# A two-call attention block with its feed-forward projections: a new deal of projection triples to slots, a score lag of four, two value visits, and earlier turns of the maxima

## Chip, cores and metric
One core of a Trainium2 chip. The metric is the device time of one execution in microseconds (us). The kernel of before took 627.68 us in the median of three runs.

## The reference, cut to what matters
The program computes two layers over `x` of shape (2, 512, 512). The change lies in the first:

```python
xn = layernorm(x)
qkv = xn @ qkv_w + qkv_b                       # 32 heads of 16, rope on q and k
s = (causal_softmax(q @ k.T / 4) @ v) @ out_w + out_b
g = silu((silu(xn @ W_gate.T) * (xn @ W_up.T)) @ W_down.T)
x = x + s * g
```

The second layer (a recurrent chain and an octonion feed-forward network) follows and is not touched.

## The kernel before
Layer one is computed in two calls, b = 0 and 1, one per sequence of 512 rows. All five engines (PE is TensorE, DVE VectorE, ACT ScalarE, POOL GpSimd, SP the DMA queue's engine) have programs of their own, written out in the same order of *slots* and tied by semaphores. Each engine works in order.

**Units and triples.** The weights come in units of 128x512: q and k of eight heads each (`Q_UNIT`, `K_UNIT`, "rope units"), four of v, 22 of the gate and up projections (`FFN_UNIT`, taking turns). A unit below 34 is multiplied in four parts, each of them three matmuls over high and low parts (L967 to L969): a *triple*, `job_part`. Units use the banks `proj_ps` alternately, so the first triple of unit u waits until the result of unit u - 2 has been read (`job_released`, L1025): for a gate or up unit by DVE's `ffn_out`, for a rope unit by ACT's `rope_copy` (three copies, L1312 to L1314). Rope units then pass DVE's `rope_times` and `rope_second`, ACT's rounding `rope_hi` (L1304), POOL's `rope_lo`, and SP, which writes them to DRAM and reads them back, arranged by heads, into `q_st` and `k_st`.

**Slots.** Heads are worked in 8 groups g of four. A group's causal scores are five tasks x = 0 to 4, so there are 40 tasks, one per slot s = 5g + x. In a slot PE does the scores of one task (`scores`, one buffer, whose row maxima DVE must have finished before the next slot's scores), the transposed scores of the task `LAG` = 5 slots earlier (`scores_T`), the triples dealt to the slot (`fill`), a turn of maxima, a turn of contexts and a value visit, as far as the slot has them. With the lag there are 45 score slots. After them come 12 slots of the down projection, which also hold what is left of the last groups.

**Maxima.** DVE writes the row maxima, POOL splits them (`join_maxima`), PE turns them into `one_turn_ps` (`max_turn`, slots with x = 3 and x = 0), and ACT copies them into two rows of `q_st` (`max_out`, L1295). The transposed scores of the same two heads read those rows, so they come out less their maximum. ACT takes the exponential (L1379), POOL clears what is above the diagonal (`keep_causal`).

**Values.** `pv_in`: in slots 5g + 11 to 5g + 14 one key tile each is multiplied into `ctx_ps`, in the next ACT copies it out, and one slot later PE turns it (`ctx_in`, slots 16, 21, ...), also into `one_turn_ps`; DVE reads that, takes the reciprocal of the sum and multiplies (L1662, L1664). `turn_banks` puts every turn of contexts and of maxima on the same bank, and a turn waits until all earlier uses of its bank are read:

```python
banks += [x % 2 if kind in ("xn", "ctxf") else 0 for kind, x in TURN]
...
if TURN_BANK[n][1]:
    pe.wait_ge(turn_done(n), TURN_BANK[n][1])
```

**Orders of ACT and DVE in a slot.** ACT: exponential, copy of contexts, `ffn_tanh` or `rope_copy` of units finished in the slot before (`units_after`), `rope_hi`, `max_out`, later splits. DVE: row maxima (L1518), contexts, `rope_second`, `rope_times`, `ffn_out`.

**The deal.** `triple_slot` gives 12 of the 112 triples of units 6 to 33 to the time ahead of slot 0 (slot -1) and shares out the rest by the room that each slot has. Slots 0 to 4 get 4, 3, 3, 4, 3, later ones mostly 2. Ahead of slot 0 stand units 6, 7 (gate and up) and 8 (Q); 9 (K) is slot 0. Rope units finish in slots -1 (8), 0 (9), 4 (12), 5 (13), 14 (18) and 16 (19). Through `unit_slot` the deal also sets when SP loads raw weights, when POOL and ACT split them (`split_in_slot`), and when rope rows are rounded, written and read.

## Time and profile before

| | us |
|---|---|
| runs, median (lowest, highest) | 627.68 (627.14, 629.33) |
| profiled execution, its own time | 627.55 |
| its span in the profile | 625.6 |
| PE busy in the span | 603.1 |
| DVE, ACT, POOL busy | 380.0, 297.6, 388.1 |
| score stage of call 0 and 1, start to start | 141.6, 139.7 |

Times in the profile are counted from the span's start. A row of the timeline has the start in us, the length in us, the engine, the line of the kernel, the operation, output<-input by name and by shape, and how many instructions are merged in it. Square brackets hold the idle time of that engine just before it and what ended it. The records of matmuls overlap, so the time that one takes is the distance to the next one's start.

### The profile page before, as it was taken

What the parts mean: (1) busy time and instruction counts of PE and PEld (TensorE: products, weight loads), DVE (VectorE), ACT (ScalarE), POOL (GpSimd) and SP (SyncE); (2) the same over time, 40 slices, a digit from 0 to 9 for tenths busy, and PEclk for the clock granted to TensorE, in tenths of its full rate; (3) what the DMA queues carried; (4) which work ended last, traced back from release to release, by engine and by line L of the source; (5) the groups of instructions that cost most, each with busy time, mean ns of one, the idle gap of its engine ahead of it and who ended that gap; (6) DMA issues with size and microseconds to landing.
All of it is one profiled execution on the core that took longest, in us unless ns stands there. A gap on an engine that the chain in (4) does not pass through costs nothing.

```text
span 625.6 us, 9856 instructions
## 1 busy us (share of the span) xinstructions
PE 603.1 (96%) x3368; PEld 418.3 (67%) x3368; DVE 380.0 (61%) x908; ACT 297.6 (48%) x460; POOL 388.1 (62%) x598
## 2 busy tenths in 40 slices
PE   6997999999999999989999999999999999999996
PEld 5875655656657888656555666688887676767664
DVE  5955868666526489667686663265986261516257
ACT  3634767555643633356665557346122344232432
POOL 6776967555334578779576544346988495731364
PEclk9998999999999999999999999999999999999999
DMA  8797684744522327667768554835410000000002
GB/s 290 242 305 220 169 237 140 222 133 110 145 67 68 102 84 205 170 187 205 208 175 231 168 144 145 312 99 187 164 73 1 0 2 1 0 1 1 0 35 101
DMA packets 60369, 83.63 MB, mean 134 GB/s; under 512 B 17936, under 2 KB 26768, under 8 KB 60320
## 3 DMA queue, kind: packets, MB, share of 16 engines
q1 hardware_dynamic: 57968, 75.02, 40.6%
q10 hardware_dynamic: 2352, 8.00, 3.4%
q8 instruction: 27, 0.44, 0.3%
q14 instruction: 22, 0.18, 0.1%
HBM read 65.17 MB, written 26.99 MB: 147 GB/s over the span
## 4 chain that ended last, share of the span: by engine, by line
PE 78%; ACT 4%; DVE 4%; issue 3%; POOL 1%; DMA 1%; POOLq 0%; SPq 0%; ACTq 0%; DVEq 0%
PE proj_ps L967 8%; PE proj_ps L969 6%; PE proj_ps L968 6%; PE ctx_ps L1123 6%; PE score_ps L997 4%; PE proj_ps L1171 3%; PE proj_ps L1172 3%; PE scoreT_ps L1006 3%; PE score_ps L967 3%; PE score_ps L969 2%; PE score_ps L968 2%; PE scoreT_ps L967 2%; PE scoreT_ps L968 2%; PE scoreT_ps L969 2%; DVE score_ps L1518 2%
## 5 line engine op out<-in xcount | busy, mean ns | idle before, releaser
L784 POOL TENSOR_TENSOR w_lo<-raw,w_hi 128x512 fp32r<-128x512 f32 x98 | 130.9, 1340 | 76.0 <-ACT w_hi L1336 70.5
L1518 DVE CUSTOM_DVE_ANT_0 score_ps<-score_ps,causal 128x512 f32<-128x512 f32 (+3 forms) x256 | 118.6, 519 | 66.1 <-PE score_ps L997 65.3
L1379 ACT ACTIVATE probs_T<-scoreT_ps 128x1024 f32<-128x1024 f32 x80 | 82.1, 1027 | 67.6 <-PE scoreT_ps L1006 66.1
L967 PE MATMUL proj_ps<-xn_hi,w_hi 128*128 128x512 f32 x224 | 98.9, 441 | 7.5 <-DVE gate_silu L1569 5.2
L969 PE MATMUL proj_ps<-xn_lo,w_hi 128*128 128x512 f32 x224 | 88.9, 397 | 0.0
L968 PE MATMUL proj_ps<-xn_hi,w_lo 128*128 128x512 f32 x224 | 88.9, 397 | 0.0
L967 PEld LDWEIGHTS proj_ps<-xn_hi,w_hi 128*128 128x128 f32 x224 | 42.2, 188 | 35.5 <-issue 23.1
L815 POOL TENSOR_SCALAR_AFFINE_SELECT probs_T<-probs_T 128x256 f32<-128x256 f32 x128 | 54.3, 448 | 5.6 <-ACT probs_T L1379 5.6
L942 POOL TENSOR_TENSOR hsL<-hidden_T,hsH 128x256 fp32r<-128x256 f32 x44 | 38.1, 884 | 26.6 <-ACT hsH L1458 26.1
L782 POOL TENSOR_SCALAR w_hi<-raw 128x512 fp32r<-128x512 f32 x50 | 33.9, 679 | 25.8 <-PE proj_ps L969 25.0
L969 PEld LDWEIGHTS proj_ps<-xn_lo,w_hi 128*128 128x128 f32 x224 | 42.4, 189 | 10.1
L1123 PE MATMUL ctx_ps<-probs_T,V 128*32 128x128 f32 (+3 forms) x512 | 47.7, 445 | 0.0
L1295 ACT ACTIVATE q_st<-one_turn_ps 2x512 fp32r<-2x512 f32 x64 | 37.5, 587 | 19.0 <-PE one_turn_ps L983 18.5
L968 PEld LDWEIGHTS proj_ps<-xn_hi,w_lo 128*128 128x128 f32 x224 | 42.5, 190 | 5.8
L997 PEld LDWEIGHTS score_ps<-k_st,q_st 50*128 50x128 f32 x256 | 20.4, 184 | 34.5 <-issue 26.3
L997 PE MATMUL score_ps<-k_st,q_st 50*128 50x512 f32 (+3 forms) x256 | 40.0, 370 | 2.1 <-DVE row_max L1518 2.1
L1336 ACT ACTIVATE w_hi<-raw 128x512 fp32r<-128x512 f32 x48 | 29.9, 624 | 21.2 <-DMA raw<-w 7.8
L950 POOL TENSOR_TENSOR inv_std<-var_eps,half 128x8 f32<-128x8 f32 x9 | 14.8, 1647 | 34.8 <-DVE var_eps L1822 34.8
L1680 DVE TENSOR_TENSOR hsl<-hidden_T,hsh 128x512 fp32r<-128x512 f32 x22 | 16.2, 735 | 32.1 <-ACT hsh L1403 32.0
L1518 DVE DVE_READ_ACCUMULATOR2_ANT row_max<- 128x1 f32 x256 | 35.7, 139 | 0.0
L805 POOL TENSOR_SCALAR max_cols<-row_max 128x8 fp32r<-128x8 f32 x32 | 8.6, 268 | 43.5 <-DVE row_max L1518 43.5
L1006 PE MATMUL scoreT_ps<-q_st,k_st 50*128 50x512 f32 (+3 forms) x256 | 34.6, 326 | 0.7 <-ACT probs_T L1379 0.4
(314 smaller groups left out, 1351.8 us busy)
## 6 DMA issues: line engine op xcount, KB each, us to landing
raw<-w SPq DMA_DIRECT2D x98, 256.0 KB, 2.9
rows<-rows_hi SPq DMA_DIRECT2D x32, 256.0 KB, 3.4
arranged<-tern SPq DMA_DIRECT2D x96, 85.0 KB
q_st<-rows SPq DMA_DIRECT2D x32, 200.0 KB
k_st<-rows SPq DMA_DIRECT2D x32, 200.0 KB
rows<-rows_lo SPq DMA_DIRECT2D x16, 256.0 KB, 4.0
gate_w<-arranged ACTq DMA_DIRECT2D x4, 704.0 KB, 6.5
up_w<-arranged ACTq DMA_DIRECT2D x4, 704.0 KB, 7.5
```

The source lines that it names most:

```text
L784: nc.gpsimd.tensor_tensor(w_lo[n % SPLIT][:, :], raw[n % RAW][:, :], F32(w_hi[n % SPLIT][:, :]), ALU.subtract).then_inc(unit_ready, 1)
L815: m = nc.gpsimd.affine_select(out=block, in_=block, pattern=[[0, 2], [1, P]], compare_op=ALU.is_ge, fill=0.0, base=0, channel_multiplier=-1)
L942: nc.gpsimd.tensor_tensor(hsL[d % HS][:, :], hidden1_T[:, f, 256 * pr:256 * pr + 256], F32(hsH[d % HS][:, :]), sub).then_inc(hs1_ready, 1)
L967: nc.tensor.matmul(acc, lh, rh, start=first, stop=False)
L968: nc.tensor.matmul(acc, ll, rh, start=False, stop=False)
L969: return nc.tensor.matmul(acc, lh, rl, start=False, stop=last)
L997: m = nc.tensor.matmul(score_ps[:, hh, c:c + (qt + 1) * P], q[:, qt * P:(qt + 1) * P], k[:, 0:(qt + 1) * P], start=part == 0, stop=True, s ...
L1006: m = nc.tensor.matmul(scoreT_ps[:, hh, c:c + S - kt * P], k[:, kt * P:(kt + 1) * P], q[:, kt * P:], start=part == 0, stop=True, skip_grou ...
L1123: m = nc.tensor.matmul(ctx_ps[32 * h:32 * h + 32, kt * P:S], V[:, kt, (4 * g + h) * 32:(4 * g + h + 1) * 32], probs_T[g % 2][x][:, h % 2, ...
L1295: m = nc.scalar.activation(q_st[g % 3][64 * hh:64 * hh + 2, j % 2, :], turn_bank(n)[32 * hh:32 * hh + 2, :], ACT.Copy)
L1379: nc.scalar.activation(probs_T[g % 2][x][:, :, :], scoreT_ps[:, :, :], ACT.Exp, scale=0.25).then_inc(probs_ready, 1)
L1518: m = nc.vector.tensor_tensor_reduce(out=block, in0=block, in1=causal[:, S - w:], scale=1.0, scalar=-3e38, op0=ALU.add, op1=ALU.max, accum ...
```

## The change
`LAG` falls from 5 to 4, so a call has 44 score slots. Units 6 and 7 become Q and K, units 8 and 9 a gate and an up unit. A function `deal` shares out the triples by a sum of what each slot holds, in units of 10 ns, with at most three as a rule, and never lets a unit begin less than two slots after the last but one has ended. Slots 0 to 4 get 3, 3, 2, 3, 3. From slot 20 to 39, those with x = 0 and x = 1 get 1, the others 2 or 3. The value product of a group is done in two visits, tile 0 in slot 5g + 10 and tiles 1 to 3 in the next; ACT copies in slot 5g + 12, and the contexts turn in slot 5g + 13. The maxima turn in front of a slot's last triple (before: behind it), so in a slot with both turns the maxima come first, and `turn_order` says so. DVE does both ropes of units 6 and 7 ahead of slot 0. Rope units now finish in slots -1 (6), -1 (7), 5 (12), 7 (13), 14 (18) and 17 (19).

```diff
--- before.py
+++ after.py
@@ -47,14 +47,14 @@
 B_TILES = [[(0, 0, 0)], [(0, 1, 0), (0, 3, 384)], [(0, 2, 0), (1, 2, 256)], [(1, 0, 0)], [(1, 1, 0), (1, 3, 384)]]
 PARTS = 5
 TASKS = PARTS * GROUPS
-LAG = 5
+LAG = 4
 SCORE_SLOTS = TASKS + LAG
 SLOTS = SCORE_SLOTS + FC + 1
 
 U_DOWN, U_OUT = 34, 45
 UNITS = U_OUT + KC
-Q_UNIT, K_UNIT, V_UNIT = (0, 8, 12, 18), (1, 9, 13, 19), 2
-FFN_UNIT = [6, 7, 10, 11, 14, 15, 16, 17] + list(range(20, 34))
+Q_UNIT, K_UNIT, V_UNIT = (0, 6, 12, 18), (1, 7, 13, 19), 2
+FFN_UNIT = [8, 9, 10, 11, 14, 15, 16, 17] + list(range(20, 34))
 IN_FRONT = 3 * KC
 FILL = 6
 TRIPLES = (U_DOWN - FILL) * KC
@@ -82,13 +82,7 @@
 
 
 def triple_slot(k):
-
-
-    room = [290 - 43 * (s < TASKS) - 33 * (s >= LAG) - 71 * (s >= 11) for s in range(SCORE_SLOTS)]
-    if k < IN_FRONT:
-        return -1
-    part = (k - IN_FRONT) * sum(room)
-    return next(s for s in range(SCORE_SLOTS) if part < (TRIPLES - IN_FRONT) * sum(room[:s + 1]))
+    return DEAL[k]
 
 
 def triples_in(s):
@@ -111,16 +105,25 @@
     return [u for u in range(FILL, U_DOWN + SPLIT) if (unit_slot(u - SPLIT) + 1 + (u >= U_DOWN) if u - SPLIT >= FILL else 0) == s]
 
 
+def rope_slot(u):
+
+    return unit_slot(u) - (u == Q_UNIT[1])
+
+
+def rounded_in(s):
+    return [u for u in sorted(QK_OF) if u >= FILL and rope_slot(u) + 3 == s]
+
+
 def rest_in_slot(s):
-    return [u for u in sorted(QK_OF) if u >= FILL and unit_slot(u) + 4 == s]
+    return [u for u in sorted(QK_OF) if u >= FILL and rope_slot(u) + 4 == s]
 
 
 def written_in(s):
-    return [u for u in sorted(QK_OF) if u >= FILL and unit_slot(u) + 5 == s]
+    return [u for u in sorted(QK_OF) if u >= FILL and rope_slot(u) + 5 == s]
 
 
 def read_in(s):
-    return next((g for g in range(1, GROUPS) if (1 if g == 1 else max(PARTS * g - 5, unit_slot(K_UNIT[g // 2]) + 7)) == s), None)
+    return next((g for g in range(1, GROUPS) if (1 if g == 1 else max(PARTS * g - 10 + LAG, unit_slot(K_UNIT[g // 2]) + 7)) == s), None)
 
 
 def down_in(s):
@@ -155,27 +158,61 @@
     return j if 0 <= j < PAIRS else None
 
 
+
+PV_VISITS = ((0,), (1, 2, 3))
+PV_FIRST = LAG + 6
+
+
 def pv_in(s):
-    g, kt = divmod(s - 11, PARTS)
-    return (g, kt) if s >= 11 and g < GROUPS and kt <= NT else None
+    g, x = divmod(s - PV_FIRST, PARTS)
+    return (g, PV_VISITS[x]) if 0 <= g < GROUPS and x < len(PV_VISITS) else None
+
+
+def pv_copied_in(s):
+    g, x = divmod(s - PV_FIRST, PARTS)
+    return g if 0 <= g < GROUPS and x == len(PV_VISITS) else None
 
 
 def ctx_in(s):
-    return (s - 16) // PARTS if s >= 16 and (s - 16) % PARTS == 0 and (s - 16) // PARTS < GROUPS else None
+    g, x = divmod(s - PV_FIRST, PARTS)
+    return g if 0 <= g < GROUPS and x == 3 else None
+
+
+def deal():
+
+
+    held = [43 * (score_in(s) is not None) + 33 * (prob_in(s) is not None) + 22 * (max_in(s) is not None) + 53 * (ctx_in(s) is not None)
+            + (sum((14, 86, 64, 43, 22)[kt + 1] for kt in (-1, *pv_in(s)[1])) if pv_in(s) else 0) for s in range(SCORE_SLOTS)]
+    triple = 70
+    length = (triple * (TRIPLES - IN_FRONT) + sum(held)) / SCORE_SLOTS
+    at, room = [-1] * IN_FRONT, 0
+    for s in range(SCORE_SLOTS):
+        room += length - held[s]
+        while len(at) < TRIPLES and (room >= triple / 2 and at.count(s) < 3 or held[s] + triple * at.count(s) < 230):
+            k = len(at)
+
+            if k % KC == 0 and at[k - KC - 1] >= max(s - 1, 0):
+                break
+            at.append(s)
+            room -= triple
+    return at + [SCORE_SLOTS - 1] * (TRIPLES - len(at))
 
 
 def turns_in(s):
     return {NORM_TURN: (0, 1), NORM_TURN + 1: (2, 3)}.get(s, ())
 
 
+DEAL = deal()
+
+
 def turn_order():
 
     at = {}
     for s in range(SLOTS):
+        if max_in(s) is not None:
+            at["max", max_in(s)] = len(at)
         if ctx_in(s) is not None:
             at["ctx", ctx_in(s)] = len(at)
-        if max_in(s) is not None:
-            at["max", max_in(s)] = len(at)
         for kc in turns_in(s):
             at["xn", kc] = len(at)
         for kc in context_in(s):
@@ -1032,8 +1069,13 @@
                     m.then_inc(proj_done, 1)
 
             def fill(b, s):
-                for k in triples_in(s):
+                triples = triples_in(s)
+                for n, k in enumerate(triples):
+                    if n == len(triples) - 1 and max_in(s) is not None:
+                        max_turn(b, max_in(s))
                     job_part(b, FILL + k // KC, k % KC)
+                if not triples and max_in(s) is not None:
+                    max_turn(b, max_in(s))
 
             pe.wait_ge(ones_set, 2)
             for n in range(WARM):
@@ -1091,8 +1133,6 @@
                             pe.wait_ge(probs_ready, TASKS * b + s - LAG)
                         scores_T(b, g, x)
                     fill(b, s)
-                    if max_in(s) is not None:
-                        max_turn(b, max_in(s))
                     if context_in(s):
                         for kc in context_in(s):
                             turn(b, ("ctxf", kc), [ctx_rows[:, t, kc * P:(kc + 1) * P] for t in range(NT)])
@@ -1111,19 +1151,20 @@
                         g = ctx_in(s)
                         pe.wait_ge(ctx_copied, GROUPS * b + g + 1)
                         turn(b, ("ctx", g), [ctx_sums[:, t * P:(t + 1) * P] for t in range(NT)])
-                    if pv_in(s) and pv_in(s)[1] < NT:
-                        g, kt = pv_in(s)
-                        if kt == 0:
+                    if pv_in(s):
+                        g, tiles = pv_in(s)
+                        if 0 in tiles:
                             pe.wait_ge(probs_masked, TASKS * b + PARTS * (g + 1))
                             pe.wait_ge(v_written, NT * (b + 1))
                             if GROUPS * b + g:
                                 pe.wait_ge(ctx_copied, GROUPS * b + g)
-                        for h in range(4):
-                            x, c = block_at(h // 2, kt)
-                            m = nc.tensor.matmul(ctx_ps[32 * h:32 * h + 32, kt * P:S], V[:, kt, (4 * g + h) * 32:(4 * g + h + 1) * 32],
-                                                 probs_T[g % 2][x][:, h % 2, c:c + S - kt * P], start=kt == 0, stop=kt == NT - 1,
-                                                 skip_group_check=True)
-                        if kt == NT - 1:
+                        for kt in tiles:
+                            for h in range(4):
+                                x, c = block_at(h // 2, kt)
+                                m = nc.tensor.matmul(ctx_ps[32 * h:32 * h + 32, kt * P:S], V[:, kt, (4 * g + h) * 32:(4 * g + h + 1) * 32],
+                                                     probs_T[g % 2][x][:, h % 2, c:c + S - kt * P], start=kt == 0, stop=kt == NT - 1,
+                                                     skip_group_check=True)
+                        if NT - 1 in tiles:
                             m.then_inc(pv_done, 1)
                     if turns_in(s):
                         pe.wait_ge(*job_released(b, JOBS - 1))
@@ -1377,8 +1418,8 @@
                             act.wait_ge(*((combined, 2 * NT * b) if b else (tern_stored, 96)))
                         act.wait_ge(scoreT_done, TASKS * b + s - LAG + 1)
                         nc.scalar.activation(probs_T[g % 2][x][:, :, :], scoreT_ps[:, :, :], ACT.Exp, scale=0.25).then_inc(probs_ready, 1)
-                    if pv_in(s) and pv_in(s)[1] == NT:
-                        g = pv_in(s)[0]
+                    if pv_copied_in(s) is not None:
+                        g = pv_copied_in(s)
                         act.wait_ge(pv_done, GROUPS * b + g + 1)
                         if g:
                             act.wait_ge(turned, use(b, ("ctx", g - 1)) + 1)
@@ -1388,9 +1429,8 @@
                             ffn_tanh(b, u)
                         else:
                             rope_copy(b, u)
-                    for u in units_after(s - 2):
-                        if u in QK_OF:
-                            rope_hi(b, u)
+                    for u in rounded_in(s):
+                        rope_hi(b, u)
                     if max_in(s) is not None:
                         max_out(b, max_in(s))
                     if parted_in(s) is not None:
@@ -1645,8 +1685,9 @@
                         nc.vector.scalar_tensor_tensor(out=tern_neg[w][:, :], in0=tern_w[w][:, :], scalar=theta[:, 1, w:w + 1], in1=tern_over[w][:, :],
                                                        op0=ALU.is_lt, op1=ALU.subtract).then_inc(tern_ready, 1)
                 for u in units_after(0):
-                    if u in FFN_OF:
-                        ffn_out(b, u)
+                    if u in QK_OF:
+                        rope_times(b, u)
+                        rope_second(b, u)
                 for s in range(SLOTS):
                     if score_in(s):
                         row_maxima(b, s)
@@ -1665,13 +1706,13 @@
                                                 c3[:, :, 0:D].rearrange("p (t h) d -> p t h d", t=NT),
                                                 rinv[:, :].rearrange("p (t h) -> p t h", t=NT).unsqueeze(3).broadcast_to([P, NT, 4, D]),
                                                 ALU.mult).then_inc(turn_done(n), 1)
-                    for u in units_after(s - 2):
+                    for u in units_after(s - 2) if s > 2 else ():
                         if u in QK_OF:
                             rope_second(b, u)
-                    for u in units_after(s - 1):
+                    for u in units_after(s - 1) if s > 1 else ():
                         if u in QK_OF:
                             rope_times(b, u)
-                    for u in units_after(s) if s else ():
+                    for u in units_after(s):
                         if u in FFN_OF:
                             ffn_out(b, u)
                     if parted_in(s) is not None:
```

## Rows read from the trace of the kernel before

**Rows 1.** The page, busy time, share, matmuls of PE.
```profile
PE 603.1 (96%) x3368; PEld 418.3 (67%) x3368; DVE 380.0 (61%) x908; ACT 297.6 (48%) x460; POOL 388.1 (62%) x598
```

**Rows 2.** Windows: stretch, length, busy of PE, PEld, DVE, ACT, POOL, clock, DMA, GB/s.
```profile
37.80:60.00 22.20, 18.72 (x80) 12.71 (x80) 14.26 (x43) 7.88 (x12) 16.07 (x18) 0.92 0.85 287
```

**Rows 3.** Timeline of PE, first scores and first down matmul of each call.
```profile
37.81 0.50 PE L997 MATMUL score_ps<-k_st,q_st 50*128 50x512 f32 x2
...
179.38 0.50 PE L967 MATMUL score_ps<-w_hi,hsh 128*128 128x512 f32 x1
...
254.29 0.49 PE L997 MATMUL score_ps<-k_st,q_st 50*128 50x512 f32 x2
...
393.96 0.50 PE L967 MATMUL score_ps<-w_hi,hsh 128*128 128x512 f32 x1
```

**Rows 4.** Timeline of PE, value visit of tile 1, then slots 15 and 16.
```profile
82.14 0.85 PE L1123 MATMUL ctx_ps<-probs_T,V 128*32 128x384 f32 x8
82.93 0.50 PE L997 MATMUL score_ps<-k_st,q_st 50*128 50x512 f32 x2
...
88.99 0.40 PE L1006 MATMUL scoreT_ps<-q_st,k_st 50*128 50x512 f32 x2
89.32 0.50 PE L967 MATMUL proj_ps<-xn_hi,w_hi 128*128 128x512 f32 x1
...
90.82 0.40 PE L983 MATMUL one_turn_ps<-ident_r,max_cols 128*34 128x128 f32 x4
91.15 0.50 PE L997 MATMUL score_ps<-k_st,q_st 50*128 50x384 f32 x4
91.48 0.45 PE L1006 MATMUL scoreT_ps<-q_st,k_st 50*128 50x384 f32 x4
91.86 0.50 PE L967 MATMUL proj_ps<-xn_hi,w_hi 128*128 128x512 f32 x1
```

**Rows 5.** Timeline of PE: waits of both fronts, a maxima turn, a context turn.
```profile
51.49 0.76 PE L967 MATMUL proj_ps<-xn_hi,w_hi 128*128 128x512 f32 x1 [2.70 <-DVE gate_silu L1569]
...
57.47 0.47 PE L967 MATMUL proj_ps<-xn_hi,w_hi 128*128 128x512 f32 x1 [0.78 <-DVE hidden_T L1573]
...
76.92 0.42 PE L983 MATMUL one_turn_ps<-ident_r,max_cols 128*34 128x128 f32 x4
...
94.33 0.63 PE L963 MATMUL one_turn_ps<-ident,ctx_sums 128*128 128x128 f32 x4 [0.27 <-ACT q_st L1295]
94.89 1.06 PE L1123 MATMUL ctx_ps<-probs_T,V 128*32 128x512 f32 x8
95.88 0.50 PE L997 MATMUL score_ps<-k_st,q_st 50*128 50x256 f32 x4
...
267.51 0.47 PE L967 MATMUL proj_ps<-xn_hi,w_hi 128*128 128x512 f32 x1 [2.25 <-DVE gate_silu L1569]
```

**Rows 6.** Timeline of ACT, max_out behind a turn, then the queue of slot 15.
```profile
77.38 1.19 ACT L1295 ACTIVATE q_st<-one_turn_ps 2x512 fp32r<-2x512 f32 x2 [1.64 <-PE one_turn_ps L983]
...
89.49 1.03 ACT L1379 ACTIVATE probs_T<-scoreT_ps 128x1024 f32<-128x1024 f32 x1 [1.64 <-PE scoreT_ps L1006]
90.41 0.59 ACT L1385 ACTIVATE ctx_sums<-ctx_ps 128x512 f32<-128x512 f32 x1
90.89 0.69 ACT L1312 ACTIVATE by_cos<-proj_ps,qk_bias 128x512 f32<-128x512 f32 x1
...
93.00 1.19 ACT L1295 ACTIVATE q_st<-one_turn_ps 2x512 fp32r<-2x512 f32 x2
```

**Rows 7.** Timeline of DVE: end of slot 16's maxima, contexts, two tensor_tensors of 512 columns.
```profile
93.19 0.14 DVE L1518 DVE_READ_ACCUMULATOR2_ANT row_max<- 128x1 f32 x1
...
94.99 0.26 DVE L1662 RECIPROCAL rinv<-one_turn_ps 128x16 f32<-128x16 f32 x1 [1.67 <-PE one_turn_ps L963]
...
95.63 0.68 DVE L1593 TENSOR_TENSOR by_cos<-by_cos,rope_cos 128x512 f32<-128x512 f32 x1
...
104.45 1.36 DVE L1605 TENSOR_TENSOR turned_rows<-by_cos,by_sin 128x512 f32<-128x512 f32 x1
```

## Prediction

> **What bounds the kernel.** The page comes first: TensorE (PE) is busy 603.1 of 625.6 us [rows 1], so only its own work and the gaps between its matmuls count. The windows by stage come second: the first slots are the one stretch with real holes and a fallen clock, 18.72 us busy in 22.20 at 0.92 [rows 2]. The timeline of PE comes third, and there I go by starts, since the records of matmuls overlap. The score stage runs from 37.81 to 179.38 (141.6 us) in call 0 and from 254.29 to 393.96 (139.7 us) in call 1 [rows 3]. Undisturbed slots give prices from start to start [rows 4]: scores 0.34, transposed scores 0.33 (0.38 with four blocks), two triples in front of a turn 1.50, so 0.70 a triple and 0.11 more for the first after other work; 0.10 more for the last where scores or a value product follow; a turn of the maxima 0.33. A turn of contexts takes 0.53 (0.56 where shown), a value product of key tile 0 1.00 and of tile 1 0.79 [rows 4, 5]; by that step of 0.21, tiles 2 and 3 take 0.57 and 0.36. Slots with one kind of scores alone pay 0.43.
>
> A call's 45 score slots then need 133.1 us: 100 triples 70.0, their firsts and lasts 7.3, 16 turns of maxima 5.3, 6 of contexts 3.2, 28 value visits 19.0, 35 paired scores 24.1, 10 alone 4.3. So PE stands still for 8.4 us of the stage in call 0 and 6.5 in call 1. These 14.9 us are all that better timing can win.
>
> **What the change does, part by part.**
>
> *Front units.* The projection of unit 12 waited for the gate_silu of unit 10, which stood on DVE behind the ropes: PE idled 2.70 us in call 0 and 2.25 in call 1, and again 0.78 in front of unit 13 [rows 5]. In call 0 the clock then fell to half; the mean of 0.92 [rows 2] is 1.8 us of clock, some 1.3 of it outside the idling. Counted from start to start, the front waits are about 5.2 and 3.4 us. With Q6 and K7 finished ahead of slot 0 they go. DVE now has two rope_times and two rope_seconds in front of its first maxima, and unit 8 waits for ACT's rope copy of Q6: I count 0.3 per call. In slot 2, with two triples, PE is through in 0.43 + 1.61 = 2.04 us, while DVE needs 93.33 - 91.15 = 2.18 from the scores' start to finished maxima [rows 4, 7] and 0.10 to PE: 0.24 lost. Unit 11 waits 0.14 for unit 9.
>
> *Work of TensorE.* In one visit, tiles 1 to 3 pay their overhead once. Tile 1 takes 0.79 where its three steps of 0.21 are 0.63; I take 0.14 per visit saved, 1.43 for the three instead of 1.72. One slot fewer pairs one more of each kind of scores. Against it, the turn of maxima now splits the triples: in 12 slots there is a first triple again, and the last one ends before scores. No row shows a triple behind such a turn; it costs nothing extra if its weights load under the turn, 0.2 if as between scores and triples with both ends. I take 0.08, near the 0.11 of a first triple. The same sum gives 133.8 us for the 44 slots, with one context turn more in them; the down stage then holds 2.8 us of value products and turns instead of 3.9. In all 0.5 us less per call, between 1.2 less and 2.5 more.
>
> *Context turns beside maxima.* This is the hard term. Both turns go to bank one_turn_ps. Before, maxima turn in slots 5g+3 and 5g, contexts in 5g+1. After, contexts turn in 5g+3 too, right behind the last triple, so they wait for max_out of the same slot, ACT's two copies of the maxima. ACT starts those 0.46 after the turn starts (76.92, 77.38), takes 1.19, and PE goes on 0.14 later (93.00 + 1.19, 94.33) [rows 5, 6]: 1.79, where PE has 0.33 + 0.78 = 1.11 to do. So 0.68 is lost in slots 13, 33 and 38. In 23 and 28 ACT comes late: exp starts 0.34 + 0.50 into the slot and takes 0.93, a tanh 0.48 (priced as the copy at 90.41) [rows 6], and 3.58 against PE's 2.63 is 0.95 each. In 18 it is the rope copy of K19, 2.10 from 90.89 [rows 6]: 0.84 + 0.93 + 2.10 + 1.19 + 0.14 = 5.20, 2.57 lost. Sum 6.5 per call. Nothing covers it: PE takes its queue in order, and the next scores, triples and value products all stand behind that turn.
>
> *Lag four.* Transposed scores read the maxima's rows of q_st. They now come in the slot right behind the turn, where a whole slot of some 3 us lay between; in exchange the turn comes one triple (0.88) sooner. With ACT free 0.24 is lost in slots 4 and 6 each, and 0.3 in slot 36 behind a tanh. With a rope ahead of max_out on ACT it is more. Slot 8 has exp, rope copy of K13, rounding of Q12 (one more copy of 512 columns, 0.48) and max_out, done for PE at 0.84 + 0.93 + 2.10 + 0.48 + 1.19 + 0.14 = 5.68; PE arrives at 0.72 + 0.80 + 0.33 + 0.88 + 0.34 = 3.07: 2.61 lost in slot 9. In slot 15 with Q18 it is 5.20 against 4.07, 1.13 in slot 16. In slot 20 the rounding of K19 waits for its rope_second on DVE, behind rope_times, ffn_out and the maxima: 2.0 lost in slot 21. Sum 6.5 per call. The next exp is queued behind max_out, so nothing of it is made up.
>
> *DVE behind the context turn.* DVE waits for that turn before it comes to ffn_out. Then 0.10 + 0.64 for reciprocal and product [rows 5, 7], 0.68 for ffn_out (as the product at 95.63) and 0.15 to PE (by 51.49) make 1.57 into the next slot, where the first triples of units 26 and 31 want their bank at 0.67: 0.9 in slots 29 and 39 each. The maxima of slot 14 come 0.2 late. With the 0.7 of the front, 2.7 per call.
>
> *DVE against POOL.* A tensor_tensor of 512 columns took 0.68 at 95.63 and 1.36 at 104.45, with POOL at a split [rows 7]. I take the short value, since POOL has little of two inputs in slots 19 and 20. The long one adds up to 1.7 in slot 21 of each call. The Trainium skill's GPSIMD Engine Reference, Key points, says that GpSimd shares its SBUF interfaces with VectorE and that DVE instructions with two SBUF inputs contend there; by that rule the long value holds wherever a split is under way, and the sum would be 3 us higher.
>
> *The rest* I put at nothing. SP's reads of group g may start six slots ahead of use instead of five. The row writes move with rope_slot and keep their distance to the reads, which also shifts SP's raw loads behind them by a slot at most, with five units split ahead. POOL's join of the maxima has half a slot or more before the turn; if a split of 1.9 us stood ahead of it in the slots with one triple, PE would wait there for a few tenths.
>
> **Sum.** The profiled execution took 627.55 us. Stalls gone: 8.4 + 6.5 = 14.9. Work: 1.0 less. New stalls: 2 x (6.5 + 6.5 + 2.7) = 31.4. 627.55 - 14.9 - 1.0 + 31.4 = 643.05. That execution lies 0.13 under the median of the runs shown, so it is 643 either way.
>
> **Rivals.**
> *A. Only the front's gain arrives: 620 us, faster.* For it: the front waits lie on PE itself, and the dealt slots are very even, 3.0 us each. Less 8.6 for the fronts, 1.4 more for the small waits left there, 1.0 less work: 619 to 621. The point that decides is whether max_out is through 1.11 us after its turn's start, and the order of ACT's queue; the rows say 1.79, with the rope copies ahead. 7%.
> *B. The new waits come to half: no change, 627.* If the waits in slots 9, 16, 18 and 21 shrink to what ACT's work exceeds a slot by (1 to 2 us less each), about 15 new stand against 16 gone. Against it: from 89.49 to 94.33, exp, copy, rope copy and max_out added up in full until PE [rows 5, 6]. 7%.
> *C. The clock falls as well: 650.* An idling of 2.70 us went with half clock in call 0, one of 2.25 did not in call 1 [rows 5]. Slots 9, 18 and 21 would idle 2.0 to 2.5 us. Six falls at 1.3 give 651, with slow ropes on DVE 654; half of them 650. The rows leave it open. [...] 16%.
> *D. The change doesn't do what it says.* The deal could leave things where they were; but slots 0 to 4 get 3, 3, 2, 3, 3 triples where they had 4, 3, 3, 4, 3, and the code carries each of the moves. Below 1%.
> The forecast itself has 70%.
>
> **How the numbers follow.** 643 is the sum of the likeliest case, whose own range is 636 to 649: each new wait a quarter smaller, or contention on DVE and 0.2 behind each turn. To hold 8 in 10 I take in most of C and stop short of B: 633 to 651. About 0.3%, 2 us, is what a measurement of this kernel can tell from no change. Faster by more: A and part of B, 9%. Within: part of B, 4%. Slower: the forecast, C and the remainder, 87%.
>
> **What would show it.** Right: PE idle in front of twelve turns of contexts, released by ACT's q_st, for 0.4 to 2.4 us; PE idle in front of transposed scores, released by q_st, in slots 9, 16 and 21 of each call; slots 29 and 39 waiting for DVE; the waits of 2.70 and 2.25 us gone and the first slots at clock 1.00; PE's busy time nearly unchanged, its score stages near 149 us each. Wrong: context turns without idling ahead of them, score stages of 137 us or less, or a new stall elsewhere, as in the down stage.

## The result and the profile after

The kernel after takes 655.39 us in the median of six runs (652.19 to 658.30), beside 628.03 us (626.06 to 629.33) for the kernel before; the ratio is 1.044, 95% interval 1.041 to 1.047. The direction was forecast, the size was not: 655.4 lies 12 us over the forecast of 643 and outside its range of 633 to 651. The profiled execution took 658.30 us, 30.75 more than the one of before.

The page and the view of the core, kernel after, which answer to [rows 1]:

```profile
core 0: 656.4 us, clock 0.976
...
PE 612.9 (93%) x3368; PEld 427.4 (65%) x3368; DVE 384.1 (59%) x908; ACT 296.6 (45%) x460; POOL 388.2 (59%) x598
```

The matmuls are as many as before, 3368, but they are busy for 9.8 us more, and the mean granted clock is 0.976 where it was 0.996. So two things were added: time in which PE stands still, and matmuls that run slower. The view by stretches has both (length, busy of PE, PEld, DVE, ACT, POOL, granted clock, DMA share, GB/s). The first two rows are the score stages of the two calls, which answer to the starts in [rows 3]; the others are three of the five stretches at half clock inside the first of them; the two left out, 71.4 to 74.8 and 180.6 to 184.0, look the same.

```profile
37.80:196.00 158.20, 142.97 (x873) 90.90 (x873) 90.95 (x306) 82.56 (x115) 87.40 (x148) 0.94 0.54 158
270.00:425.60 155.60, 138.60 (x874) 87.59 (x873) 92.35 (x306) 82.58 (x115) 86.73 (x147) 0.97 0.56 160
...
44.10:47.50 3.40, 3.40 (x10) 2.19 (x10) 1.21 (x8) 0.00 (x0) 2.45 (x3) 0.50 0.71 229
...
108.90:115.70 6.80, 6.80 (x24) 4.48 (x22) 4.33 (x14) 1.51 (x2) 2.27 (x6) 0.50 0.84 255
146.50:149.90 3.40, 3.40 (x9) 2.60 (x9) 1.84 (x9) 0.26 (x1) 0.77 (x3) 0.50 0.83 233
```

The same view of the kernel before:

```profile
37.80:179.40 141.60, 135.64 (x870) 84.87 (x869) 92.35 (x308) 86.12 (x118) 90.14 (x150) 0.99 0.62 179
254.30:394.00 139.70, 134.37 (x870) 84.04 (x869) 91.74 (x308) 86.12 (x118) 88.63 (x149) 1.00 0.62 178
```

Length less busy is PE's idle time: 6.0 and 5.3 us before, 15.2 and 17.0 us after, 20.9 more. The five stretches at 0.50 (1.2 instead of 2.4 GHz) are 20.5 us long in all; with PE busy in all of them, half of that is lost. Three more in call 1 (276.2, 303.5 and 351.3, 10.2 us) bring the loss to 15.3 us, where the one stretch of before had cost 1.4 outside its idle time. The score stages grew by 32.5 us: 20.9 of idle time, 13.9 of clock, and the remainder, 2.3 less, is work at full clock. Outside them 1.8 went, which makes the 30.7 more of the profiled execution. **The forecast had 15.5 for the sum, and nothing in it for a falling clock.**

Where PE stood, in the view of waits of the kernel after, first call 0, then call 1 (waited for: us in total, times, longest):

```profile
PE one_turn_ps L1000 <- ACT q_st L1336: 6.1, 6, 2.5
PE scoreT_ps L1043 <- ACT q_st L1336: 4.3, 3, 2.5
PE score_ps L1034 <- DVE row_max L1558: 2.6, 1, 2.6
PE proj_ps L1004 <- DVE hidden_T L1613: 0.8, 1, 0.8
PE proj_ps L1004 <- DVE gate_silu L1609: 0.8, 1, 0.8
```

```profile
PE one_turn_ps L1000 <- ACT q_st L1336: 6.1, 6, 2.5
PE scoreT_ps L1043 <- ACT q_st L1336: 5.2, 3, 2.5
PE score_ps L1034 <- DVE row_max L1558: 3.5, 1, 3.5
...
```

Six turns of contexts (L1000) per call wait for ACT's copy of the maxima (L1336), three transposed scores (L1043) wait for the same copy, and two triples (slots 29 and 39) wait for DVE: those rows were forecast. The third row is the one that was not. The first tall one, slot 18, in the timelines of PE and ACT (start, length, [idle before it]):

```profile
105.64 0.40 PE L1006 MATMUL proj_ps<-xn_lo,w_hi 128*128 128x512 f32 x1
108.54 0.73 PE L1000 MATMUL one_turn_ps<-ident,ctx_sums 128*128 128x128 f32 x4 [2.50 <-ACT q_st L1336]
```

```profile
104.20 1.03 ACT L1420 ACTIVATE probs_T<-scoreT_ps 128x1024 f32<-128x1024 f32 x1 [0.34 <-PE scoreT_ps L1043]
105.12 0.68 ACT L1353 ACTIVATE by_cos<-proj_ps,qk_bias 128x512 f32<-128x512 f32 x1
105.81 0.68 ACT L1354 ACTIVATE by_sin<-proj_ps,qk_bias 64x512 f32<-64x512 f32 x1
106.51 0.68 ACT L1355 ACTIVATE by_sin<-proj_ps,qk_bias 64x512 f32<-64x512 f32 x1
107.21 1.18 ACT L1336 ACTIVATE q_st<-one_turn_ps 2x512 fp32r<-2x512 f32 x2
```

ACT works without a pause from the exponential to the end of the maxima at 108.39, and PE goes on 0.15 later. So the wait is for ACT's queue; with the maxima copied first (below) it is 0.61 us instead of 2.50. Half clock begins at 108.9, right behind it.

The wait that was not forecast, slot 1 of call 0, on DVE and POOL:

```profile
34.42 1.14 DVE L1633 TENSOR_TENSOR by_cos<-by_cos,rope_cos 128x512 f32<-128x512 f32 x1 [3.11 <-ACT by_sin L1355]
35.48 1.78 DVE L1634 TENSOR_TENSOR by_sin<-by_sin,rope_sin 128x512 f32<-128x512 f32 x1
37.35 0.69 DVE L1645 TENSOR_TENSOR turned_rows<-by_cos,by_sin 128x512 f32<-128x512 f32 x1
37.96 1.10 DVE L1633 TENSOR_TENSOR by_cos<-by_cos,rope_cos 128x512 f32<-128x512 f32 x1
38.98 1.77 DVE L1634 TENSOR_TENSOR by_sin<-by_sin,rope_sin 128x512 f32<-128x512 f32 x1
40.84 0.92 DVE L1645 TENSOR_TENSOR turned_rows<-by_cos,by_sin 128x512 f32<-128x512 f32 x1
41.69 0.68 DVE L1558 CUSTOM_DVE_ANT_0 score_ps<-score_ps,causal 128x512 f32<-128x512 f32 x1
```

```profile
37.74 0.77 POOL L819 TENSOR_SCALAR w_hi<-raw 128x512 fp32r<-128x512 f32 x1 [1.04 <-DMA raw<-w]
38.60 1.60 POOL L821 TENSOR_TENSOR w_lo<-raw,w_hi 128x512 fp32r<-128x512 f32 x1
```

The scores of slot 0 started at 37.79, but their maxima only at 41.69. The six products of Q6 and K7 fill DVE from 34.42 on, 7.3 us. They take up to 1.1 and 1.8 us where POOL splits a weight (w_lo, as at 38.60), and 0.69 where it does not (37.35); six at 0.69 would be 4.1 us, and the 3.2 above that are more than the wait. This is read from the rows: no run took the splits away. The scores of slot 1 waited 2.55 us in call 0 and 3.46 in call 1.

### The profile page after: what moved, and what is told of

Same layout as the page of the kernel before. It is cut to its first block, busy times and chain, and to the rows that moved or that the text cites. A ratio compares the mean times of both kernels' runs of the same rounds, so it can differ in the third digit from the quotient of the medians.

```text
span 656.4 us, 9856 instructions
## 1 busy us (share of the span) xinstructions
PE 612.9 (93%) x3368; PEld 427.4 (65%) x3368; DVE 384.1 (59%) x908; ACT 296.6 (45%) x460; POOL 388.2 (59%) x598
## 4 chain that ended last, share of the span: by engine, by line
PE 49%; ACT 4%; DVE 2%; issue 2%; POOL 1%; POOLq 0%; DVEq 0%; ACTq 0%
PE proj_ps L1004 4%; PE proj_ps L1212 3%; PE proj_ps L1213 3%; PE proj_ps L1006 3%; PE proj_ps L1005 3%; PE ctx_ps L1164 3%; PE score_ps L1034 2%; ACT q_st L1336 2%; PE scoreT_ps L1043 2%; PE ctx_ps L1212 2%; PE scoreT_ps L1212 2%; PE scoreT_ps L1213 2%; PE ctx_ps L1213 2%; PE one_turn_ps L1291 1%; POOL hsL L979 1%
## 5 line engine op out<-in xcount | busy, mean ns | idle before, releaser
L821 POOL TENSOR_TENSOR w_lo<-raw,w_hi 128x512 fp32r<-128x512 f32 x98 | 134.7, 1379 | 68.9 <-ACT w_hi L1377 63.4
L1004 PE MATMUL proj_ps<-xn_hi,w_hi 128*128 128x512 f32 x224 | 102.5, 458 | 3.4 <-DVE hidden_T L1613 1.6
L1006 PE MATMUL proj_ps<-xn_lo,w_hi 128*128 128x512 f32 x224 | 92.6, 414 | 0.0
L1005 PE MATMUL proj_ps<-xn_hi,w_lo 128*128 128x512 f32 x224 | 92.5, 413 | 0.0
L1004 PEld LDWEIGHTS proj_ps<-xn_hi,w_hi 128*128 128x128 f32 x224 | 44.3, 198 | 24.6 <-issue 8.8
L852 POOL TENSOR_SCALAR_AFFINE_SELECT probs_T<-probs_T 128x256 f32<-128x256 f32 x128 | 50.9, 421 | 13.5 <-ACT probs_T L1420 13.5
L1006 PEld LDWEIGHTS proj_ps<-xn_lo,w_hi 128*128 128x128 f32 x224 | 44.6, 199 | 11.0
L1005 PEld LDWEIGHTS proj_ps<-xn_hi,w_lo 128*128 128x128 f32 x224 | 44.6, 199 | 5.7
L1043 PE MATMUL scoreT_ps<-q_st,k_st 50*128 50x512 f32 (+3 forms) x256 | 35.9, 336 | 10.0 <-ACT q_st L1336 9.5
L1164 PE MATMUL ctx_ps<-probs_T,V 128*32 128x128 f32 (+3 forms) x512 | 42.4, 450 | 0.0
L1336 ACT ACTIVATE q_st<-one_turn_ps 2x512 fp32r<-2x512 f32 x64 | 37.2, 582 | 7.0 <-PE one_turn_ps L1020 5.7
```

Source lines behind the costliest of these rows:

```text
L821: nc.gpsimd.tensor_tensor(w_lo[n % SPLIT][:, :], raw[n % RAW][:, :], F32(w_hi[n % SPLIT][:, :]), ALU.subtract).then_inc(unit_ready, 1)
L852: m = nc.gpsimd.affine_select(out=block, in_=block, pattern=[[0, 2], [1, P]], compare_op=ALU.is_ge, fill=0.0, base=0, channel_multiplier=-1)
L1004: nc.tensor.matmul(acc, lh, rh, start=first, stop=False)
L1005: nc.tensor.matmul(acc, ll, rh, start=False, stop=False)
L1006: return nc.tensor.matmul(acc, lh, rl, start=False, stop=last)
L1043: m = nc.tensor.matmul(scoreT_ps[:, hh, c:c + S - kt * P], k[:, kt * P:(kt + 1) * P], q[:, kt * P:], start=part == 0, stop=True, skip_grou ...
```

## The experiments

For each execution, span times (1 - granted clock) estimates the time lost to half clock. The table gives its median as "clock lost", and the median of the time without it as "at full clock". It is an upper estimate, since it also counts half clock while PE stands: behind the last matmul that is 0.6 us in the profiled execution of the kernel before and 0.7 in that of the kernel after. The ratio is to the kernel before, run on the same chip beside it.

| kernel | us, median (range) | ratio [95%] | at full clock | clock lost |
|---|---|---|---|---|
| before | 628 (30 runs, 625.9 to 630.0) | 1 | 625.5 | 2.5 |
| after | 655.39 (652.19 to 658.30) | 1.044 [1.041, 1.047] | 641.5 | 13.4 |
| lag five in after | 624.28 (623.63 to 627.11) | 0.995 [0.992, 0.997] | 620.0 | 4.4 |
| lag four in before | 649.38 (646.19 to 650.72) | 1.035 [1.033, 1.038] | 642.1 | 6.5 |
| contexts turned later | 650.29 (647.90 to 652.23) | 1.035 [1.031, 1.038] | 635.6 | 14.9 |
| old front in after | 651.58 (648.96 to 653.45) | 1.037 [1.034, 1.040] | 639.4 | 13.0 |
| PE kept busy | 653.25 (649.40 to 654.78) | 1.038 [1.034, 1.042] | 644.3 | 8.8 |
| maxima copied first | 639.49 (635.25 to 640.12) | 1.017 [1.014, 1.020] | 631.9 | 7.0 |
| front mended, lag four | 651.60 (650.12 to 653.24) | 1.038 [1.035, 1.041] | 639.5 | 12.4 |
| front mended, lag five | 620.65 (619.77 to 622.39) | 0.989 [0.987, 0.991] | 619.8 | 0.9 |
| all three repairs, lag four | 635.39 (632.56 to 637.25) | 1.011 [1.008, 1.014] | 630.0 | 5.7 |
| maxima turned last, lag five | 621.32 (619.75 to 622.95) | 0.989 [0.987, 0.991] | 619.4 | 1.9 |
| four visits, lag five | 624.23 (623.47 to 625.84) | 0.994 [0.992, 0.995] | 621.5 | 2.5 |
| maxima copied first, lag five | 633.16 (630.72 to 634.36) | 1.008 [1.005, 1.010] | 628.8 | 4.1 |

**Lag five in the kernel after.**

```diff
-LAG = 4
+LAG = 5
```

> The changed kernel with the lag back at five slots, all else kept (front units, deal, two visits, maxima in front of the last triple). Theory 1, ACT's copy of the maxima is the cause: the contexts now turn in slots 5g+14, without maxima beside them, and transposed scores come two slots after their maxima. The waits in front of context turns (7.4 us per call), in front of the transposed scores of slots 9, 16 and 21 (4.8) and the DVE waits of slots 29 and 39 (1.8) all go, and most of the falls of the clock with them: 655.4 - 28 - 8 = about 620, in any case under 628. Theory 2, the front units are the cause: the front is untouched, so the time stays over 645. Theory 3, contention and splitting of triples cost everywhere: over 640.

It took 624.28 us, some 31 us under the kernel after and 0.5% under the kernel before. Call 0 in the view of waits:

```profile
PE score_ps L1034 <- DVE row_max L1558: 3.7, 4, 2.8
PE proj_ps L1004 <- DVE hidden_T L1613: 1.0, 2, 0.8
PE proj_ps L1004 <- ACT by_sin L1355: 0.6, 1, 0.6
...
```

The rows of q_st are gone, those of the context turns too, since PV_FIRST follows the lag and contexts then turn a slot behind the maxima. The wait of slot 1 for DVE stands (2.8). So the lag, with the context turns that move along with it, carries the slowdown, and everything else in the change together is a small gain.

**Lag four in the kernel before**, value visits one slot earlier, contexts turned where they were.

```diff
-LAG = 5
+LAG = 4
...
-    g, kt = divmod(s - 11, PARTS)
-    return (g, kt) if s >= 11 and g < GROUPS and kt <= NT else None
+    g, kt = divmod(s - 10, PARTS)
+    return (g, kt) if s >= 10 and g < GROUPS and kt <= NT else None
```

> The kernel before with the lag of four alone (value visits one slot earlier with it; front, deal rule, four value visits and the turn of maxima behind the last triple as before). The transposed scores then stand one scores' work (0.34) behind the turn: each of the 16 copies of maxima per call is waited for, 1.79 - 0.67 = 1.1 us, more where a rope is ahead on ACT. If the lag is the cause in the changed kernel: 628 + 2 x (16 x 1.1 + some 4) and falls of the clock, 665 to 680, slower than the changed kernel, whose earlier turn gives part back. If the lag is harmless and the visits, the deal or the split triples are the cause: within 628 to 632.

It took 649.38 us: slower, but well short of the 665 to 680 put on record, and 6 us faster than the kernel after, where it was expected slower. Call 0:

```profile
PE scoreT_ps L1006 <- ACT q_st L1295: 7.3, 11, 1.3
PE proj_ps L967 <- DVE gate_silu L1569: 4.7, 2, 2.9
PE score_ps L997 <- DVE row_max L1518: 0.4, 1, 0.4
```

Eleven transposed scores wait for the maxima instead of three, since the turn stands behind the last triple here; but each for 0.3 to 1.3 us, seven of them for 0.5 or less, where 1.1 had been put. A triple of slot 8 waits 1.79 for gate_silu, which is new as well. In all, PE idles 24.3 us in the two score stages where it idled 11.3, 13.0 more. The table has 642.1 - 625.5 = 16.6 at full clock; the records show each wait shorter than it is from start to start (by 0.16 for those of transposed scores), and the rest was not taken apart.

**Contexts turned one slot later.** A second edit, not shown, keeps the deal unchanged.

```diff
     g, x = divmod(s - PV_FIRST, PARTS)
-    return g if 0 <= g < GROUPS and x == 3 else None
+    return g if 0 <= g < GROUPS and x == 4 else None
```

> The changed kernel with the turn of contexts one slot later (5g+14), lag four and the same deal. If the shared bank is what costs, the waits of the context turns go (2 x 0.79 x 3 and 2 x 1.03 x 2, and of slot 18's 2.67 the 1.1 beyond what the next transposed scores would wait anyway), and slots 29 and 39 lose their 0.9: 2 x 7.3 = 14.6 us less, with one to three falls of the clock 638 to 641. The lag's waits in slots 9, 16 and 21 stay. If DVE or the lag were behind those waits, they would only move to the next slot: 652 or more.

650.29 us, 5 under the kernel after where 14 to 17 were expected. Call 0:

```profile
PE scoreT_ps L1043 <- ACT q_st L1336: 7.2, 5, 2.5
PE score_ps L1034 <- DVE row_max L1558: 3.3, 2, 2.4
...
```

The context turns wait no more (6.1 before the edit), nor do slots 29 and 39 for DVE. But the waits for q_st in front of transposed scores grew from 4.3 to 7.2: ACT's late copy had been waited for twice, and PE now meets it at the next instruction (slot 19 waits 1.97, slot 21 2.10 where it had waited 0.82). DVE, held by the later turn, is late in slot 21 too (0.88). The clock fell as much as before (14.9 lost). A wait that stands in front of another, for the same late engine, is not worth its own length.

**The front units of before in the kernel after.**

```diff
-Q_UNIT, K_UNIT, V_UNIT = (0, 6, 12, 18), (1, 7, 13, 19), 2
-FFN_UNIT = [8, 9, 10, 11, 14, 15, 16, 17] + list(range(20, 34))
+Q_UNIT, K_UNIT, V_UNIT = (0, 8, 12, 18), (1, 9, 13, 19), 2
+FFN_UNIT = [6, 7, 10, 11, 14, 15, 16, 17] + list(range(20, 34))
```

(with rope_slot and DVE's loops as before)

> The changed kernel with the front units of before (gate and up first, then Q8 and K9), lag, deal rule, visits and turns as changed. If the new front is worth its old waits (8.6 us), this is slower than the changed kernel: 660 to 662. If the new front has only traded the wait for gate_silu against one for the first maxima behind four rope operations on DVE (2.7 and 3.6 us, each with a fall of the clock), it comes out even: 651 to 656.

651.58 us: the old front is 4 us better than the new one here (2 at full clock), and of the 2.70 us for the gate_silu of unit 10 [rows 5] only 0.78 returns, in slot 4 (0.83 from start to start, behind 1.24 for the maxima in front of slot 3's scores). So most of that wait went without the new order of the units. The kernel before with lag four, which keeps the old deal, still waits 2.95 and 2.24 us there. That points to the even deal, 3, 3, 2, 3, 3 triples for 4, 3, 3, 4, 3; no run changed the deal alone.

**PE kept busy in front of three waits**: unused matmuls ahead of the waits of slots 1, 9 and 18 in the kernel after.

```diff
+            def keep_busy(n):
+                for _ in range(n):
+                    nc.tensor.matmul(ctx_ps[:, :], ident_r[:, :], xn_hi[:, 0, :], start=True, stop=True)
...
+                        if s == 1:
+                            keep_busy(11)
...
+                        if s == 9:
+                            keep_busy(10)
...
+                        if s == 18:
+                            keep_busy(10)
```

> The changed kernel with idle matmuls (into ctx_ps, which is free there, result unused) in front of the three longest waits of each call: 11 of 512 columns ahead of slot 1's scores, 10 ahead of slot 9's transposed scores, 10 ahead of slot 18's context turn. They wait out the same events, so no wait is shorter. If falls of the clock cost what the forecast lacked, at least four of the falls go and the time drops by 5 to 9 us: 647 to 650, granted clock 0.985 or more. If the clock follows from something else, time and clock stay: 655, 0.976 to 0.98.

653.25 us, 2 under the kernel after with overlapping ranges, and above what was expected. No half clock followed slots 1, 9 and 18 any more, but it came at 142.3 and 371.0 (slot 29 of both calls), 176.4 and 405.1 (slot 39 of both) and 343.7 (slot 21): the pauses there are those of the kernel after, and two of these five had brought no fall there. The table has 4.6 less of clock lost and 2.8 more at full clock, 1.1 of it a wait for the rows of k in slot 0 that the kernel after doesn't have; the rest was not taken apart. So padding some pauses moves part of the falls to others, and is no repair.

**The maxima copied first on ACT**, in the kernel after.

```diff
+                    if max_in(s) is not None:
+                        max_out(b, max_in(s))
                     for u in units_after(s):
                         if u in FFN_OF:
                             ffn_tanh(b, u)
                         else:
                             rope_copy(b, u)
                     for u in rounded_in(s):
                         rope_hi(b, u)
-                    if max_in(s) is not None:
-                        max_out(b, max_in(s))
```

> The changed kernel with one change of order on ACT: in a slot, the copy of the maxima comes ahead of tanh, rope copies and rounding. If ACT's queue is what makes the long waits, slot 18's context turn waits 0.67 instead of 2.56, slot 9's transposed scores 0.2 instead of 2.3, slots 16 and 21 next to nothing, slots 23 and 28 0.67 instead of 0.92; the plain 0.67 of the shared bank stays, as do slots 29 and 39. That is 12 us, and with fewer falls of the clock 634 to 638. If the bank alone were the cause: 652 or more. If DVE's ropes pay for the later rope copies, between the two.

639.49 us, 1.5 over the expected range and 16 under the kernel after. Waits of call 0, then both score stages by stretches:

```profile
PE one_turn_ps L1000 <- ACT q_st L1336: 3.7, 6, 0.6
PE proj_ps L1004 <- ACT by_sin L1355: 2.5, 2, 1.7
...
```

```profile
39.10:181.90 142.80, 133.63 (x873) 84.99 (x873) 88.29 (x305) 83.05 (x114) 87.22 (x148) 1.00 0.61 177
256.00:406.70 150.70, 139.73 (x874) 88.97 (x873) 90.03 (x306) 83.64 (x115) 87.40 (x148) 0.95 0.58 165
```

The transposed scores wait no more; all six context turns wait the 0.6 us that the copy needs with ACT free, as forecast for three of them. In exchange a unit's bank waits for its rope copy (1.7 in slot 9). The second fence is the cleanest view of the clock: two calls of one program, idle 9.2 and 11.0 us. The first kept 2.4 GHz and took 142.8 us; the other had four stretches of half clock, 13.7 us in all, and took 150.7. PE was busy 6.1 us longer for the same matmuls.

**Only Q6's rope ahead of slot 0 on DVE**, with lag five and with lag four.

```diff
                 for u in units_after(0):
-                    if u in QK_OF:
+                    if u == Q_UNIT[1]:
                         rope_times(b, u)
                         rope_second(b, u)
...
-                    for u in units_after(s - 2) if s > 2 else ():
-                        if u in QK_OF:
+                    for u in units_after(s - 2):
+                        if u in QK_OF and u != Q_UNIT[1]:
                             rope_second(b, u)
-                    for u in units_after(s - 1) if s > 1 else ():
-                        if u in QK_OF:
+                    for u in units_after(s - 1):
+                        if u in QK_OF and u != Q_UNIT[1]:
                             rope_times(b, u)
```

> The changed kernel with lag five, and on DVE only Q6's rope ahead of slot 0; K7's rope_times comes in slot 1 and its rope_second in slot 2, behind the maxima. If the wait of slot 0 in the run with lag five alone (2.9 and 2.5 us) is due to four rope operations in DVE's queue, it goes, for up to 1.2 us of a new one in slot 2: 620 to 622, against 624.3 there. If it has another cause (POOL or DMA), 624 stays.

> The changed kernel with lag four as changed and the same repair of the front on DVE. The waits of slot 0 (2.6 and 3.5 us) shrink by some 4 us in all, and two falls of the clock (1.5 us each) with them: 648 to 650. If the rest of the excess is ACT's copy of the maxima, all its waits are still there, unchanged in length.

620.65 us with lag five, 1.1% under the kernel before and the best of all; 651.60 with lag four, a little over its expectation. K7's products now stand behind the maxima of slots 1 and 2. Lag five, call 0:

```profile
PE score_ps L1034 <- DVE row_max L1558: 2.0, 4, 1.2
PE proj_ps L1004 <- DVE hidden_T L1613: 1.7, 3, 0.8
```

The longest wait for DVE fell from 2.8 to 1.2 us. At full clock that is only 620.0 to 619.8; the rest of the 3.6 us is clock, 4.4 lost against 0.9.

**All three repairs at lag four** (front, copy first, contexts later), to see how much of the lag's price is order.

> The kernel after, lag four kept, with three repairs at once: only Q6's rope ahead of slot 0 on DVE, the copy of the maxima ahead of tanh and rope copies on ACT, and the turn of contexts one slot later. Theory (what lag four costs is ACT's order and the shared bank, both of which a planner can move): the run with the copy first alone took 639.5 us; its waits ahead of turns of contexts and behind them (.67 six times, .78 three times, 1.77 in slot 9 stays) go for 2 x 6.4 us, its front waits of 2.0 and 2.5 stay at about 2.0, and some of the waits of slots 20 and 21 seen with the later turn alone (0.95 and 1.89) may come: 626 to 631. Rival (lag four itself costs, by the maxima being needed one slot after the scores, whatever stands ahead on ACT): 635 or more. Rival (falls of the clock follow any remaining wait): the idling goes but two to four low stretches per call stay, 633 to 638.

635.39 us: above the 626 to 631 of the theory, at the lower edge of the first rival (the lag itself costs) and inside the range of the second (the clock falls after what waits are left), and there is something of both. No wait for q_st is left in the view of waits of call 0, but that view leaves out pauses under 0.15 us. In the timeline, 17 transposed scores in slots behind a turn of maxima (8 in call 0, 9 in call 1) still start some 0.6 us after the scores ahead of them, where 0.34 is the rule (slot 4 of the kernel after, shown in the next part, looks the same). That is 0.25 each, 4.2 us in all, with ACT as early as it can be; at lag five it does not occur. Besides there are two waits of 1.7 for rope copies (slots 9 and 19), and for DVE 0.9 in slot 21 and 1.0 in slot 29, and half clock came four times. With two turns of maxima in five slots, max_out and the units' copies compete for ACT; one order makes the maxima late, the other the banks. At full clock that is still 4.5 us over the kernel before, and 10.2 over the best at lag five.

**The turn of maxima behind the last triple again**, in the best kernel.

```diff
                 for n, k in enumerate(triples):
-                    if n == len(triples) - 1 and max_in(s) is not None:
-                        max_turn(b, max_in(s))
                     job_part(b, FILL + k // KC, k % KC)
-                if not triples and max_in(s) is not None:
+                if max_in(s) is not None:
                     max_turn(b, max_in(s))
```

> The best kernel so far (lag five, only Q6's rope ahead of slot 0; 620.7 us) with the turn of the maxima back behind a slot's last triple. Theory (the earlier turn is nearly neutral at lag five: a turn inside the triples takes 0.24 us where it took 0.33, but splits them): 619.5 to 623, so a ratio to the kernel before of 0.987 to 0.993. Rival (the earlier turn brings much of the gain of 7 us, by having the maxima's rows out sooner): 624 or more.

621.32 us, the same as without it (0.989 both): at lag five the earlier turn is worth nothing that can be measured.

**Four value visits again**, in the best kernel.

```diff
-PV_VISITS = ((0,), (1, 2, 3))
+PV_VISITS = ((0,), (1,), (2,), (3,))
...
-    g, x = divmod(s - PV_FIRST, PARTS)
-    return g if 0 <= g < GROUPS and x == 3 else None
+    g, x = divmod(s - PV_FIRST - 5, PARTS)
+    return g if 0 <= g < GROUPS and x == 0 else None
```

> The best kernel so far (lag five, only Q6's rope ahead of slot 0; 620.7 us) with each key tile of a value product visited in its own slot again, and the turn of contexts behind them as in the kernel before. Theory (three tiles in one visit take 1.43 us where they took 1.72, in 7 groups of two calls): 0.29 x 14 = 4.1 us more, 623.5 to 626. Rival (other slots' lengths decide, and PE's overheads do not add): 621 or less.

624.23 us, 3.6 more (2.8 by the ratios), where 4.1 was expected: the two visits are a real gain, near the size of their overhead. The turn of contexts moves with them, so the pair was measured. In the timeline of the kernel after, tiles 1 to 3 take 1.44 us from start to start, the sum of the prediction (1.43):

```profile
81.30 1.50 PE L1164 MATMUL ctx_ps<-probs_T,V 128*32 128x384 f32 x24
82.74 0.50 PE L1034 MATMUL score_ps<-k_st,q_st 50*128 50x256 f32 x4
```

**The maxima copied first at lag five**, in the best kernel, with the edit shown above.

> The best kernel so far (lag five, only Q6's rope ahead of slot 0; 620.7 us) with the copy of the maxima ahead of tanh and rope copies on ACT. At lag four this order was worth some 12 us. Theory (at lag five the maxima have a whole slot to spare, and the order only makes units' banks come free 1.2 us later: in slot 9 PE already waits 0.38 for such a copy): 622 to 626. Rival (ACT's order costs wherever maxima are turned, lag or not): 617 to 619.

633.16 us, 12.5 over the best kernel, 7 over the expected range and the opposite of what the same edit does at lag four. PE and ACT in slot 9:

```profile
66.67 0.45 PE L1043 MATMUL scoreT_ps<-q_st,k_st 50*128 50x384 f32 x4
69.13 0.47 PE L1004 MATMUL proj_ps<-xn_hi,w_hi 128*128 128x512 f32 x1 [2.01 <-ACT by_sin L1355]
```

```profile
65.70 1.19 ACT L1336 ACTIVATE q_st<-one_turn_ps 2x512 fp32r<-2x512 f32 x2
66.91 0.69 ACT L1353 ACTIVATE by_cos<-proj_ps,qk_bias 128x512 f32<-128x512 f32 x1
...
68.31 0.68 ACT L1355 ACTIVATE by_sin<-proj_ps,qk_bias 64x512 f32<-64x512 f32 x1
```

Counted from the exponential's start, the unit's bank comes free 1.4 us later, 1.2 of it the copy of the maxima, and the wait of 0.59 in the best kernel is 2.01; slots 21 and 30 wait some 1.5 and 1.15 us more for DVE. The maxima, copied early, are waited for by nobody. At full clock 9.0 of the 12.5 are waits, 3.2 are clock.

## Why the prediction missed

**The waits for ACT were right.** The context turns beside maxima were put at 6.5 us per call: measured from start to start they lost 0.68, 2.56, 0.92, 0.92, 0.67 and 0.67, 6.4. The lag's own waits were put at 6.5 as well, and they lost 5.6 in call 0 and 6.4 in call 1. Slots 9 and 16 were put at 2.61 and 1.13 and lost 2.66 and 1.13. Slot 21, put at 2.0, lost 0.99 and 1.84. The small ones of slots 4, 6 and 36, put at 0.24, 0.24 and 0.3, lost 0.25, 0.26 and 0.28; no view of waits shows them, only the starts. Slots 29 and 39 lost the 0.9 each that they were put at. In slot 4, then in slot 9:

```profile
52.80 0.51 PE L1034 MATMUL score_ps<-k_st,q_st 50*128 50x384 f32 x4
53.39 0.49 PE L1043 MATMUL scoreT_ps<-q_st,k_st 50*128 50x512 f32 x2
...
67.50 0.51 PE L1034 MATMUL score_ps<-k_st,q_st 50*128 50x384 f32 x4
70.50 0.50 PE L1043 MATMUL scoreT_ps<-q_st,k_st 50*128 50x512 f32 x2 [2.49 <-ACT q_st L1336]
```

**The front was mis-sized, twice.** "I count 0.3 per call" for DVE ahead of its first maxima was 2.6 and 3.5. What failed there is the choice of the short value in "DVE against POOL": the 0.68 of 95.63 instead of the 1.36 of 104.45 [rows 7], with a reason given for slots 19 and 20 only, while POOL splits weights all through the front, and six such products stood in a row. The rule cited there from the Trainium skill's GPSIMD Engine Reference, Key points, fits this trace: 1.1 to 1.8 us with a split alongside, 0.69 without. And "with Q6 and K7 finished ahead of slot 0 they go" named the smaller part: the old front in the new deal waits 0.78 there instead of 2.70 (0.78 and 2.25 in call 1).

**Two errors cancel, which is luck.** New waits were put at 31.4 us; from start to start they come to 35.7 (front 3.0 and 3.9, contexts 6.4 and 6.4, lag 5.6 and 6.4, DVE behind the context turns 2.0 and 2.0). The front, put at 0.7 a call with its small waits, is 5.5 too few; the lag is 1.0 too many. The work term took the difference of 4.3 back. It was put at 1.0 less; of the 30.75 more in the profiled execution, take off 15.3 of half clock and 35.7 of waits and add the 14.9 gone, and work is some 5.3 less. Of that, 1.8 lies outside the score stages. Most of the rest is the turn of maxima: amid the triples it takes 0.24 from start to start where 0.33 was put, 2.9 us in 32 turns, and the triple behind it 0.85 where 0.88 was put. So at full clock the kernel went from 625.5 to 641.5, 16.0 more, where the forecast had 15.5.

**The clock is the step that failed.** It stood as rival C at 16%, and the forecast itself put it at nothing in its sum, with no reason but that the rows left it open. The table has 13.4 us lost against 2.5, 10.9 of the 27.4. That it is a cause and no mere companion shows in repeats of one program: over the six executions of the kernel after, the granted clock was 0.974 to 0.983 and the time without the loss stayed within 640.8 and 642.5, while the times spread over 6 us. C was also too small. "Six falls at 1.3" was eight at 1.9: four of the six named waits were followed by half clock (slot 9 twice, 18 and 21 once), the wait of slot 1 both times, and slots 29 and 39 once each, which were on no list. They idle only 0.77, but 0.87 or 0.61 stands some 2 us earlier:

```profile
144.28 0.63 PE L1000 MATMUL one_turn_ps<-ident,ctx_sums 128*128 128x128 f32 x4 [0.87 <-ACT q_st L1336]
...
146.40 0.69 PE L1004 MATMUL proj_ps<-xn_hi,w_hi 128*128 128x512 f32 x1 [0.77 <-DVE gate_silu L1609]
```

At 146.5 the clock halves, as the stretches above show. The 1.3 had been read from one fall whose low stretch lay partly in idle time [rows 2]; the eight here lay in busy time, 3.4 us each and 6.8 once, so half of that was lost. The Trainium skill's TensorE: Matmul & The Clock Gate, HAM oscillation, tells of a loop that waits some 3 to 5 us for a DMA at every tile and is throttled again each time. This trace agrees that waits can do it again and again, but here shorter ones did it too: the pauses last ahead of the eight falls were 0.77 to 3.46 us, and not every pause of that size was followed by one.

**What stays open.** Which pause is followed by a fall: nearly the same waits brought none in call 0 of the kernel with maxima copied first and four in call 1 (those at the stage's start differ, 1.3 and 0.6 us against 2.4). The falls are placed in one profiled execution per kernel. Of the 10.2 us that three repairs at lag four leave over the best kernel at full clock, 4.2 are the small waits shown above; the rest was read from waits and not taken apart.

## What to carry to other kernels

Work out a shorter lag as a chain: what the late engine has queued ahead of the result, against what PE has left to do. At lag four, what waits for a copy of 1.2 us on ACT cost 21 us at full clock in two calls, and a better order of that queue with two more repairs brought back 11.5 of them. Give pauses of PE a second price from the start: 16 us added at full clock came with 4.0 more of lost clock in one kernel (lag four in before) and with 10.9 in another (after), so a forecast that counts idle time alone is a lower end. And take the contended duration of a neighbour wherever POOL works through a list at that moment; the short one has to be earned.

The order of an engine's queue has no best form of its own: the same swap brought 16 us at lag four and cost 12.5 at lag five. The best version found keeps the new deal and the two visits, with lag five and K7's rope behind the first maxima: 620.65 us, 1.1% under the kernel before.
